# Another order of coupled query tiles in a convolution and attention kernel

## What is computed

```python
x = _L0_conv_ref(x, w_qkv, b_qkv, temperature, w_proj, b_proj)   # channel attention
t = _to_tokens(x)                                                # (32, 1024, 192)
t = t + _L1_attn_ref(_ln_t(t), Wq, Wk, Wv)
t = t + _L1_ffn_ref(_ln_t(t), W1, b1, W2, b2)
...
att = jnp.einsum('bqhd,bkhd->bhqk', q, k) * scale
att = jnp.where(causal, att, -jnp.inf)
att = jax.nn.softmax(att, axis=-1)
out = jnp.einsum('bhqk,bkhd->bqhd', att, v)
```

## Time and profile before

| | us |
|---|---|
| median of 3 runs | 4501.67 |
| lowest, highest | 4501.24, 4506.31 |
| the profiled execution | 4509.63 |
| its span | 4507.80 |
| one image of the attention stage, steady | 102.8 |
| from the last unit's mask in a group to the first feed-forward matmul | 10.2 |

### The profile page before, as it was taken

The page is one execution under the profiler, slowest core; times in us unless marked ns, Lnnn a source line. Parts: engine busy times, 40 slices in busy tenths (PEclk is TensorE's granted clock), DMA queues, the critical chain, the costliest instruction groups (busy, mean ns, idle before and its releaser), DMA issues.

```text
span 4507.8 us, 114786 instructions
## 1 busy us (share of the span) xinstructions
PE 4014.6 (89%) x39240; PEld 2916.3 (65%) x39240; DVE 3041.2 (67%) x5559; ACT 2974.6 (66%) x6669; POOL 364.2 (8%) x375
## 2 busy tenths in 40 slices
PE   6999999879999898999989879999898999999887
PEld 4767665666777646767665667777646777664665
DVE  5666666766666677666666766666676666666765
ACT  3676666657777655676666657776655666666666
POOL 1000002000000110000002000000110000002000
PEclk7999999989999999999999989999999999999999
DMA  2111111011221101111111011221101111111011
GB/s 72 37 37 37 44 37 29 0 51 37 51 50 37 37 0 43 37 37 37 44 37 29 1 51 37 53 48 37 37 0 43 37 37 41 40 37 29 0 43 43
DMA packets 48832, 161.01 MB, mean 36 GB/s; under 512 B 12612, under 2 KB 13126, under 8 KB 48198
## 3 DMA queue, kind: packets, MB, share of 16 engines
q1 hardware_dynamic: 48326, 154.40, 14.2%
HBM read 28.52 MB, written 25.17 MB: 12 GB/s over the span
## 4 chain that ended last, share of the span: by engine, by line
PE 65%; DVE 13%; issue 12%; ACT 6%; POOL 1%; DMA 1%; DVEq 1%; ACTq 1%; SPq 0%; POOLq 0%
PE PT L698 11%; PE OUT L718 10%; PE S L684 6%; DVE nmax L1231 5%; PE PT L824 5%; PE S L743 5%; PE S L794 3%; PE S L642 3%; PE FR L642 3%; PE FR L586 2%; ACT work L952 2%; DVE work L385 2%; DVE XT L1100 2%; PE FR L649 1%; PE S L649 1%
## 5 line engine op out<-in xcount | busy, mean ns | idle before, releaser
L1231 DVE TENSOR_REDUCE nmax<-S 128x1 f32<-128x256 f32 (+7 forms) x1536 | 1146.1, 753 | 940.4 <-PE S L686 930.3
L952 ACT ACTIVATE work<-S,nmax 128x256 f32<-128x256 f32 (+7 forms) x1536 | 1138.8, 742 | 611.8 <-DVE nmax L1231 592.3
L698 PE MATMUL PT<-ident,work 128*128 128x128 f32 x6912 | 1079.3, 280 | 92.9 <-DVE work L385 57.0
L698 PEld LDWEIGHTS PT<-ident,work 128*128 128x128 f32 x6912 | 750.7, 143 | 260.0 <-ACT work L952 54.4
L385 DVE COPY work<-PT 128x512 f32<-128x512 f32 x768 | 524.0, 682 | 45.3 <-PE PT L698 38.0
L944 ACT ACTIVATE work<-PT 128x256 f32<-128x256 f32 (+3 forms) x768 | 338.7, 441 | 155.3 <-PE PT L698 148.3
L684 PE MATMUL S<-KS,QS 128*128 128x512 f16 (+3 forms) x1152 | 325.5, 337 | 109.2 <-ACT work L952 75.6
L684 PE MATMUL S<-odd 128*128 128x512 f16 (+3 forms) x1152 | 316.2, 329 | 71.7 <-ACT work L952 68.0
L686 PE MATMUL S<-causal,identb 128*128 128x128 bf16 x1536 | 339.5, 221 | 0.0
L956 ACT ACTIVATE work<-PT 128x512 f32<-128x512 f32 (+3 forms) x768 | 332.9, 433 | 1.5 <-PE PT L698 1.4
L743 PE MATMUL S<-odd,W1b 128*128 (+1 forms) x1080 | 262.1, 395 | 49.9 <-ACT work L995 41.5
(11 more groups left out here) (209 smaller groups left out, 6010.4 us busy)
## 6 DMA issues: line engine op xcount, KB each, us to landing
X<-in_x SPq DMA_DIRECT2D x32, 768.0 KB, 5.3
odd<-hi_z SPq DMA_DIRECT2D x128, 192.0 KB, 4.2
odd<-odd SPq DMA_DIRECT2D x128, 192.0 KB, 4.3
out_y<-work SPq DMA_DIRECT2D x64, 384.0 KB, 3.7
QS<-hi_z SPq DMA_DIRECT2D x64, 192.0 KB, 3.8
QS<-odd SPq DMA_DIRECT2D x64, 192.0 KB, 4.0
KS<-hi_z SPq DMA_DIRECT2D x64, 192.0 KB, 4.5
KS<-odd SPq DMA_DIRECT2D x64, 192.0 KB, 4.7
```

Source lines behind the costliest of these rows:

```text
L698: last = tr(bank[:, P * (j - c0):P * (j - c0) + P], PS[m % 2][:, m // 2 % 2, P * j:P * j + P], ident[:, :])
L952: A(PS[n % 2][:, n // 2 % 2, 0:w], S[:, n % 2, 0:w], ACT.Exp, bias=nmax[:, n % MAXES:n % MAXES + 1], accum_out=rowsum[:, sum_col(n):sum_co ...
L1231: v.tensor_reduce(nmax[:, n % MAXES:n % MAXES + 1], S[:, n % 2, 0:P * (qtile(n) + 1)], AX.X, ALU.max, negate=True).then_inc(max_made, 1)
```

## The change

The four pairs are coupled and ordered in another way. The pairs (1, 7), (3, 5), (0, 6), (2, 4) become (2, 4), (0, 6), (1, 5), (3, 7). Two pairs, (2, 4) and (0, 6), are as before and move to the first 12 units of each 24; tiles 1, 7, 3 and 5 are coupled otherwise and come in the second 12.

```diff
-TILES = [(1, 7), (3, 5), (0, 6), (2, 4)]
+TILES = [(2, 4), (0, 6), (1, 5), (3, 7)]
```

## The result

| | before | after |
|---|---|---|
| median, us | 4502.23 | 4436.01 |
| lowest, highest, us | 4501.24, 4506.31 | 4434.23, 4437.13 |
| ratio, 95% interval | | 0.985 (0.9836 to 0.9864) |
| span of the profiled execution, us | 4507.8 | 4434.0 |
| one steady image, us | 102.80 | 100.95 |

The kernel is 1.5% faster: 66 us where 52 were forecast, inside the range. The image is faster by 1.85 us where 1.8 were forecast. (Of the 73.8 us between the two spans, some 7 belong to the profiled execution of before, which was that much above its median. In the sessions of the other runs the kernel before took 4502.99 to 4504.72 us, so that a difference between two sessions is good to some 2 us.)

What follows compares the result with a forecast made beforehand. TensorE, busy 89%, was taken as the bound, so gains come only from its idle time. About -1.8 us per image over 31 images (-56) and +4 at group ends gave -52 us: 4450 us, range 4424 to 4502.

Steps and rivals of the forecast that it cites:

- A: Units 24 to 31, where pair (1, 7) gives way to (2, 4): TensorE's 3.7 us of idle time falls by 1.9.
- B: Units 12 to 19, where (0, 6) becomes (1, 5): shorter and new waits sum to 0 (ends -0.4 and +0.5 us).
- C: Unit 44 to unit 5 of the next image, (3, 7) now ending the image: 0 (ends -0.3 and +0.9 us).
- D: Units 33 and 34, tile 6 in place of tile 5 at unit 33: +0.05 us per image.
- the rest of the chain is unchanged: VectorE in A: copies and layer norm keep their time, while narrower maxima take 1.33 us off its chain.
- The work term: In A, TensorE gets 0.78 us more transposes, scores and PV products to do, which reduces its stall.
- the walk: Second estimate of A, unit by unit: stalls of about 2.0 of 3.7 us remain, so -1.7 us.
- Rival 1: ScalarE falls behind at pair (3, 7) in C: +1.1 us per image, 4540 us; chance 0.13.
- Rival 2: The stalls only move, what A gains comes back in B and C: 4500 us; chance 0.13.
- Rival 3: In A only VectorE's chain counts, no exp stall left, B gains 0.4 us: -2.5 per image, 4424 us; chance 0.14.
- The ends: After a group's last unit, tile 7 last lengthens the drain by 0.72 us, six times: +4 us (0 to +8).
- the two sums of 2.7: Waits beyond cover over four pairs, without front or PV work: 2.7 us for old and new, coupling gives nothing.

Runs made afterwards that it cites:

- order_only: Kernel before with its pairs kept and only their order changed, to (2, 4), (0, 6), (3, 5), (1, 7): 4452.14 us, ratio 0.9883.
- swap_last: Changed kernel with its last two pairs exchanged, giving (2, 4), (0, 6), (3, 7), (1, 5): 4483.71 us.
- after_round_late: Changed kernel with VectorE's second layer-norm cast moved one slot later, behind the max of unit 30: 4429.80 us.
- before_dve38: Kernel before with one added, unused VectorE reduction ahead of the max of unit 38 of each image: 4504.26 us, ratio 1.0005.

## Why the prediction was right

**The bound and the method.** That a gain can only come from TensorE's idle time, and that it lies in A, held. A's stall was forecast to fall by 1.9 us and fell by 1.84 (time less work), or by 1.5 in the idle rows. The other stretches were forecast to cancel and did in sum, but not one by one: by the idle rows B and C fell by 0.3 and 0.4 us where 0 was forecast, and D rose by 0.5. That the image came out at -1.85 for a forecast of -1.8 is partly luck.

**A, the terms.** The transposes of unit 28 were to come 1.0 us earlier; measured from the mask of unit 24 they came 0.54 earlier (352.88 - 340.17 = 12.71, before 363.05 - 349.80 = 13.25). The failed piece is "the rest of the chain is unchanged": the second cast grew by 0.42 us. The work term held: TensorE had 0.75 us more to do there, and order_only and swap_last, with 0.7 and 1.66 us less of it and a stretch as long, keep 52 and 21 us of the 66. The forecast had it as a side of the sum and did not see it as the main one. In the walk, 0.8 us was forecast before the score of unit 29 (0.49 measured), 0.7 for the transposes of slot 29 (0.80), 0.4 in slot 31 (0.72, the cast again), nothing at the transposed output (nothing).

**B.** Forecast 0. The new wait of the score of unit 15 was forecast at 0.7 and is there with 0.54, that of unit 17 went from 1.0 to 0.70 as forecast, and the softmax from 1.3 to 1.04 (-0.15 forecast); the 0.3 that the small waits were to lose together they lost:

```profile
317.82 0.50 PE L684 MATMUL S<-KS,QS 128*128 128x512 f16 x2 [0.54 <-ACT work L952]
...
320.45 0.50 PE L684 MATMUL S<-KS,QS 128*128 128x512 f16 x2 [0.70 <-ACT work L952]
```

In sum -0.3 by the idle rows, within the ends given.

**C.** Forecast 0. The score of unit 47 was to wait 0.7 to 0.9 us and that of unit 5 0.2 to 0.5:

```profile
386.37 0.61 PE L684 MATMUL S<-KS,QS 128*128 128x512 f16 x2 [0.77 <-ACT work L952]
```

```profile
295.39 0.45 PE L684 MATMUL S<-KS,QS 128*128 128x512 f16 x2 [0.25 <-ACT work L952]
```

**D** was forecast at +0.05 and rose by 0.5 to 0.6 us: the score of unit 35 waits 0.65 us for the exp of unit 33, and the first of the Q and K steps 0.2 for ScalarE.

```profile
357.86 1.01 ACT L952 ACTIVATE work<-S,nmax 128x896 f32<-128x896 f32 x1 [0.58 <-DVE nmax L1231]
```

```profile
359.01 0.55 PE L684 MATMUL S<-KS,QS 128*128 128x512 f16 x2 [0.65 <-ACT work L952]
```

The exp of unit 33 does not stand behind ScalarE's copies, as it did in the kernel before: ScalarE is idle for 0.58 us ahead of it, until its max is made. What failed is the step that priced tile 6 alone, by its 0.24 us more of wait, and not the cover. Between the scores of units 33 and 35 TensorE had ten blocks of transposes and a score of four blocks before and has eight and one now, 0.42 us less by the prices of the earlier trace rows. The two make 0.66 us, measured are 0.54 (from 0.11 to 0.65).

**Rival 1**, ScalarE behind at (3, 7), did not happen where it was feared: before the exp of unit 45 ScalarE still waited for the max.

```profile
385.11 1.11 ACT L952 ACTIVATE work<-S,nmax 128x1024 f32<-128x1024 f32 x1 [0.22 <-DVE nmax L1231]
```

swap_last took the heavy pair out of this place, and the kernel got slower, not faster. **Rival 2**, the stalls only move, is refuted by the sum over the image. **Rival 3**, -2.5 per image and no stall left by exp in A, did not come: the score of unit 29 still waits 0.49 us for an exp, and even with the cast that does not wait (after_round_late) the image is only 2.15 us below that of the kernel before.

**The ends.** 0.7 us a drain were forecast, +4 us in all, and nothing at the beginning of a group. The drain did get longer, by more: from the last unit's mask in the second group to the first feed-forward matmul (L794) it is 10.42 us before and 11.59 after, and from the last mask of all to the end 21.16 and 22.35. The first mask of the next group comes 0.4 to 1.2 us later behind the last one of a group, 3.7 us in the five; with the 1.2 at the end that is 4.9, so the term of +4 was about right.

The term put at nothing is the one that was wrong. The first image of a group gains more than the steady 1.85 us: in the second group it takes 105.22 us before and 101.00 after, 2.4 us above a steady image before and 0.05 after. Of these 4.2 us, 2.5 stand in units 0 to 11 and 2.9 in A and D, less what the other stretches take back. The six first images (five groups and the last two images) lose 30 us between the two profiles, where six times 1.85 is 11; some 5 of the 19 beyond that belong to the slower profiled execution of before (25 us instead of 30 against the profile of before_dve38, whose time is that of the kernel before). The groups hide it: from a group's first mask to its first feed-forward matmul the second group saves 11.4 us (from 931.89 to 1566.28 before, from 916.21 to 1539.20 after), about six images at 1.85, and that is a longer drain under a better beginning. No run isolates what in the first image is better.

The last image, without a front, was forecast as equal by the two sums of 2.7, and is 2.7 us faster (74.35 against 77.08). The sums hold roughly where they were meant, before the score of the last unit of a pair: four stalls of 1.20, 0.45, 1.29, 0.45 us before (3.4) and 0.59, 1.21, 0.86, 0.44 after (3.1). The rest of TensorE's idle time there went from 3.0 to some 2.1 us in 24 units, mostly before transposes that wait for copies; which of VectorE's and ScalarE's steps is behind that was not tried. So the 14 us beyond the forecast are the first images and the last one, and a part may be the width of the measured interval (61 to 74 us).

## What to carry to other kernels

Where one engine's chain has a fixed length in some stretch, count what the bound engine can do under it: work moved under the chain is saved, work moved out of it is paid in full elsewhere, so the heavy item belongs just ahead of the stretch and the light ones inside. Before taking work from the engine that seems to set a stretch, look at the order of its instructions: moving steps that could come later one slot on, behind a copy that TensorE waited for, gave more (36 us, 6 of which the late cast gives by itself) than taking two casts off the engine altogether (12 us). A time that shrinks by less than the work removed points to a second chain of about the same length, or to a wait that stands ahead of what was removed. And a kernel of repeated images has first and last ones: look at them apart from the steady one.

## What the runs showed of the hardware

A VectorE cast of 128 x 768 from fp32 to fp16 in SBUF takes 0.55 us alone and 1.03 or 1.45 us when it starts while a GpSimd instruction of 1.59 us runs on the same tiles; in both kernels it ends 0.4 us behind that instruction, though it starts 0.4 us earlier against it in one of them. VectorE's reductions of 128 x 640 from PSUM in the same time were not lengthened (0.82 us at 349.76, and 0.82 at 341.63 with GpSimd idle). And the busy time of TensorE in the profile is not its work alone: the same instructions show 94.69 us busy in an image before and 94.09 after, while the image fell by 1.85 us and the idle time by 1.3. So about 0.6 us of waits or slower starts must have been counted as busy before; the rows don't show where. (A few records of matmuls can be missing, the counts are 1023 and 1020.)
